# Expert stage of a token tower: the next group's rows turned, rounded and split in the middle of the gate products, and the scatters placed singly

## The reference

```python
logits = x @ router_w.T
routing_weights, selected = sparsemixer_eval(logits, JITTER_EPS)      # two experts a token
...
dense_w = dense_w.at[tok, selected[:, 0]].add(routing_weights[:, 0])
dense_w = dense_w.at[tok, selected[:, 1]].add(routing_weights[:, 1])
out = jnp.zeros_like(x)
for e in range(E):
    h = jax.nn.silu(x @ w_gate[e].T) * (x @ w_up[e].T)
    out = out + dense_w[:, e:e + 1] * (h @ w_down[e].T)
```

## Time and profile before

| | us |
|---|---|
| median of 3 runs | 2599.9 (2595.83 to 2601.3) |
| the profiled execution | 2601.53 |
| its span, first to last instruction | 2599.8 |
| PE busy in the span | 2218.6 |
| DVE / ACT / POOL busy | 1842.9 / 1715.3 / 1743.4 |
| mean granted clock of TensorE | 0.93 of full speed |

### The profile page before, as it was taken

One profiled execution on the slowest core, in us unless ns is written; L12 is line 12 of the kernel. 1 busy time (PEld: TensorE's weight loads), 2 busy tenths in 40 slices (PEclk: granted clock), 3 DMA queues, 4 the chain that ended last, 5 costly groups with the idle time before them and its releaser, 6 DMA issues. The chain is left out here.

```text
span 2599.8 us, 37397 instructions
## 1 busy us (share of the span) xinstructions
PE 2218.6 (85%) x11394; PEld 1850.5 (71%) x11394; DVE 1842.9 (71%) x3736; ACT 1715.3 (66%) x3574; POOL 1743.4 (67%) x1528
## 2 busy tenths in 40 slices
PE   0177578999999999999999999999999993838885
PEld 0064436887878788787888878788888882728885
DVE  2656457788878778887878878778787773465553
ACT  3433306787777878787787777878878783216663
POOL 4145507878787777878778787877777774017884
PEclk9975568999999999999999999999999997759998
DMA  9856717244343334524234442313312203426776
GB/s 380 336 200 221 243 38 201 70 98 123 86 121 81 94 93 95 136 73 124 75 94 107 96 133 54 80 40 63 68 30 56 47 14 92 139 85 191 197 197 174
DMA packets 199860, 314.81 MB, mean 121 GB/s; under 512 B 95915, under 2 KB 130219, under 8 KB 186731
## 3 DMA queue, kind: packets, MB, share of 16 engines
q1 hardware_dynamic: 189947, 298.23, 40.5%
q0 software_dynamic: 9712, 14.18, 2.9%
HBM read 210.20 MB, written 101.75 MB: 120 GB/s over the span
## 5 line engine op out<-in xcount | busy, mean ns | idle before, releaser
L1419 POOL TENSOR_TENSOR p_lo<-prob,p_hi 128x512 fp32r<-128x512 f32 (+3 forms) x1056 | 1211.4, 1166 | 376.7 <-ACT p_hi L1503 352.5
L1501 ACT ACTIVATE prob<-ps_s 128x512 f32<-128x512 f32 (+4 forms) x1344 | 726.9, 541 | 347.2 <-DVE ps_s L1741 169.3
L1503 ACT ACTIVATE p_hi<-ps_s 128x512 fp32r<-128x512 f32 (+3 forms) x1344 | 727.1, 541 | 1.6
L1638 DVE TENSOR_REDUCE max_part<-ps_x 128x1 f32<-128x512 f32 x744 | 506.4, 686 | 55.7 <-PE ps_x L1550 46.2
L1636 DVE CUSTOM_DVE_ANT_0 ps_x<-ps_x,before 128x128 f32<-128x128 f32 x496 | 244.3, 493 | 33.9 <-PE ps_x L1550 25.6
L1603 PE MATMUL ps_o<-p_hi,v_lat 128*128 128x512 f32 (+3 forms) x640 | 244.2, 382 | 17.5 <-POOL p_lo L1419 17.2
L1603 PE MATMUL ps_o<-p_hi,v_win 128*128 128x512 f32 (+3 forms) x640 | 237.1, 371 | 3.4 <-POOL p_lo L1419 3.4
L1605 PE MATMUL ps_o<-p_lo,v_win 128*128 128x512 f32 (+3 forms) x640 | 235.2, 368 | 0.0
L1605 PE MATMUL ps_o<-p_lo,v_lat 128*128 128x512 f32 (+3 forms) x640 | 234.4, 366 | 0.0
L1741 DVE TENSOR_TENSOR ps_s<-ps_s,mask_kq 128x128 f32<-128x128 f32 x512 | 153.6, 300 | 110.9 <-PE ps_s L1522 104.2
L1419 DVE TENSOR_TENSOR p_lo<-prob,p_hi 128x512 fp32r<-128x512 f32 (+1 forms) x224 | 191.3, 854 | 46.0 <-ACT p_hi L1503 40.2
(11 more groups left out here) (433 smaller groups left out, 5796.4 us busy)
## 6 DMA issues: line engine op xcount, KB each, us to landing
raw<-in_experts_w_dram SPq DMA_DIRECT2D x23, 1536.0 KB, 7.4
wbuf<-in_tok_weight_dram SPq DMA_DIRECT2D x16, 2000.0 KB, 16.9
head_first<-kw_scratch SPq DMA_DIRECT2D x72, 256.0 KB, 5.0
kw_scratch<-st_hi SPq DMA_DIRECT2D x48, 256.0 KB, 2.3
kw_scratch<-st_lo SPq DMA_DIRECT2D x48, 256.0 KB, 3.0
q_scratch<-st_hi SPq DMA_DIRECT2D x48, 256.0 KB, 3.2
q_scratch<-st_lo SPq DMA_DIRECT2D x48, 256.0 KB, 3.8
head_first<-q_scratch SPq DMA_DIRECT2D x48, 256.0 KB, 5.8
```

Of the source, the lines that this page charges most:

```text
L1419: ns.tensor_tensor(upper if low else p_lo[:, i % LSLOTS, c:CH], prob[low:P, i % NPROB, c:CH], upper.bitcast(F32), ALU.subtract).then_inc(s ...
L1501: nc.scalar.activation(prob[low:P, i % NPROB, c:CH], ps_s[i % 3][low:P, c:CH], ACT.Exp, scale=SCALE).then_inc(s["p_full"], 1)
L1503: nc.scalar.activation(p_hi[:, i % SLOTS, c:CH], ps_s[i % 3][:, c:CH], ACT.Exp, scale=SCALE).then_inc(s["p_up"], 1)
L1638: ins = nc.vector.tensor_reduce(mpart[:, q, c:c + 1], bank[:, 0:w], axis=AX.X, op=ALU.max)
```

## The change

Three things are moved; nothing is added to or taken from what is computed.

- The transposes for group i + 1, and with them `upper_x` and `lower_x`, move from the end of group i to before its third block (f = 2), on PE, ACT and DVE.
- `upper_gate` and `lower_gate` for group i + 1 move one block later: f = 1, 2 and 3 do blocks 0, 1 and 2, and block 3 follows behind the last `hm` (DVE) or before the last `h_hi` (ACT).
- `scatter` handles one half (q), and waits for that half's `yw` alone. The two scatters of group i - 2 are issued in group i behind the second and the third `h_lo`; before, those of group i - 1 stood together at the end of group i. The last two groups' scatters come together at the end, as before.

```diff
--- before.py
+++ after.py
@@ -2170,14 +2170,13 @@
                                                  in_offset=bass.IndirectOffsetOnAxis(ap=g.slot_tok[:, n:n + 1], axis=0)
                                                  ).then_inc(s[f"xg{i % 2}"], 16)
 
-            def scatter(i):
-                pool.wait_ge(s["yw"], HT * (i + 1))
-                for q in range(HT):
-                    n = HT * i + q
-                    if i:
-                        pool.wait_ge(s[f"add{q}"], 16 * i)
-                    nc.gpsimd.indirect_dma_start(out=g.acc_dram[q], out_offset=bass.IndirectOffsetOnAxis(ap=g.slot_tok[:, n:n + 1], axis=0),
-                                                 in_=yw[:, i % 2, q, :], in_offset=None, compute_op=ALU.add).then_inc(s[f"add{q}"], 16)
+            def scatter(i, q):
+                pool.wait_ge(s["yw"], HT * i + q + 1)
+                n = HT * i + q
+                if i:
+                    pool.wait_ge(s[f"add{q}"], 16 * i)
+                nc.gpsimd.indirect_dma_start(out=g.acc_dram[q], out_offset=bass.IndirectOffsetOnAxis(ap=g.slot_tok[:, n:n + 1], axis=0),
+                                             in_=yw[:, i % 2, q, :], in_offset=None, compute_op=ALU.add).then_inc(s[f"add{q}"], 16)
             gather(0)
             gather(1)
             for i in range(NTL):
@@ -2187,9 +2186,11 @@
                     nc.gpsimd.tensor_tensor(h_lo[:, i % 2, f, :], hm[:, n % 2, :], h_hi[:, i % 2, f, :].bitcast(F32), ALU.subtract).then_inc(s["lo"], 1)
                     if f == 0 and i + 2 < NTL:
                         gather(i + 2)
-                if i:
-                    scatter(i - 1)
-            scatter(NTL - 1)
+                    if f in (1, 2) and i >= 2:
+                        scatter(i - 2, f - 1)
+            for i in (NTL - 2, NTL - 1):
+                for q in range(HT):
+                    scatter(i, q)
 
         @block.tensor
         def _(pe):
@@ -2208,6 +2209,8 @@
                 pe.wait_ge(s["xlo"], i + 1)
                 pe.wait_ge(s["wlo"], gate_split(i, 3))
                 for f in range(FB):
+                    if f == 2 and i + 1 < NTL:
+                        x_transposes(i + 1)
                     n = FB * i + f
                     cols = slice(f * P, (f + 1) * P)
                     for ps, m, sem, free in ((ps_g, 0, "g", "silu"), (ps_u, 2, "u", "hm")):
@@ -2236,8 +2239,6 @@
             x_transposes(0)
             for i in range(NTL):
                 gate_up(i)
-                if i + 1 < NTL:
-                    x_transposes(i + 1)
                 if i:
                     down(i - 1)
             down(NTL - 1)
@@ -2281,6 +2282,8 @@
                 upper_gate(0, f)
             for i in range(NTL):
                 for f in range(FB):
+                    if f == 2 and i + 1 < NTL:
+                        upper_x(i + 1)
                     n = FB * i + f
                     act.wait_ge(s["g"], n + 1)
                     if n >= 2:
@@ -2290,11 +2293,11 @@
                         upper_down(i)
                     if f:
                         upper_h(i, f - 1)
-                    if i + 1 < NTL:
-                        upper_gate(i + 1, f)
+                    if f and i + 1 < NTL:
+                        upper_gate(i + 1, f - 1)
+                if i + 1 < NTL:
+                    upper_gate(i + 1, FB - 1)
                 upper_h(i, FB - 1)
-                if i + 1 < NTL:
-                    upper_x(i + 1)
                 if i:
                     weigh(i - 1)
             weigh(NTL - 1)
@@ -2318,6 +2321,8 @@
                 lower_gate(0, f)
             for i in range(NTL):
                 for f in range(FB):
+                    if f == 2 and i + 1 < NTL:
+                        lower_x(i + 1)
                     n = FB * i + f
                     dve.wait_ge(s["silu"], n + 1)
                     dve.wait_ge(s["u"], n + 1)
@@ -2326,10 +2331,10 @@
                     nc.vector.tensor_tensor(hm[:, n % 2, :], sg[:, n % 2, :], ps_u[n % 2][:, 0:TOK], ALU.mult).then_inc(s["hm"], 1)
                     if f == 0:
                         lower_down(i)
-                    if i + 1 < NTL:
-                        lower_gate(i + 1, f)
+                    if f and i + 1 < NTL:
+                        lower_gate(i + 1, f - 1)
                 if i + 1 < NTL:
-                    lower_x(i + 1)
+                    lower_gate(i + 1, FB - 1)
             for j in range(NJ):
                 c = slice(4 * j, 4 * j + 4)
                 dve.wait_ge(s[f"fin{j}"], 16 * HT)
```

## The result

| | before | after |
|---|---|---|
| median, us | 2602.06 (9 runs, 2595.83 to 2603.23) | 2609.24 (9 runs, 2606.55 to 2612.15) |
| ratio to before | 1 | 1.0031, 95% interval 1.002 to 1.0041 |
| profiled execution's span, us | 2599.8 | 2607.1 |

The changed kernel is slower by 0.31%: 8 us by the ratio, 7.2 between the medians. That is more than the 0.2% that a measurement tells from nothing, and small.

A forecast was written before the change was run, and what follows sets the result against it. POOL's round with DVE/POOL port exclusion was taken as the bound: 8.88 + 1.14 + 0.38 + 0.26 = 10.66, taken as 10.6 against 10.54 us a group. With the ends, +2.2 us on the median 2599.9: 2602, range 2581 to 2616.

The forecast's parts named there:

- What bounds the group: Expert stage: PE waits through a loop that closes over POOL, which is idle only 1.04 of 10.54 us a group.
- POOL's own work, 8.88: POOL's h_lo's, gathers and scatters with gaps, without exclusion, after the change: 8.88 us a group.
- The three collisions of the main case: POOL waits for DVE's two-operand splits: 1.14 us at a group's first h_lo, 0.38 and 0.26 at the gathers.
- main case: Steady group as summed: 10.6 us against 10.54, gate products at 2.57 after the second h_lo's start; chance 0.52.
- The collision at the last split: DVE's split for f = 3 against the h_lo behind the first scatter: split goes first, 0.10 us ahead, costing nothing.
- A: Zero of the group's clock in the forecast: the start of a group's second h_lo on POOL, in us.
- second rival: The h_lo behind the first scatter takes the port ahead of the last weight split: +15 us, 2615; chance 0.22.
- The Trainium skill's rule: A two-SBUF-input DVE instruction and a GpSimd one reading SBUF contend for ports: group stays at 10.6, without it 9.3.
- First rival, exclusion no dearer than before: Large split meets POOL inside a scatter, so POOL loses about 0.68: 9.56 us a group, 2582; chance 0.26.
- Costed at nothing: Moved transposes (0.35 us on PE either way), weight loads, scatter and yw waits add no time.
- The ends of the stage: Intervals outside the steady pace: first with scatters -0.7, last whole +0.7, last group +0.9, first two +0.1 each.
- the case without any exclusion: Within the faster rival: PE's 9.32 us a group is the bound, 19 x -1.22 + 1, giving 2579.

The follow-up runs named there:

- e3: Changed kernel with DVE's weight splits reading a zero tile in PSUM in place of the rounded weights; 0.9892 of before, 9.16 us a group.
- e10: Changed kernel with the PSUM zero tile as second operand in the last weight split (f = 3) alone; 0.9999 of before, 10.47 us a group.
- e7: Changed kernel with the two single scatters behind the third and fourth h_lo instead of the second and third; 0.9955 of before, 9.82 us a group.
- e11: Changed kernel with the PSUM zero tile as second operand in the large split (down block) alone; 1.0006 of before, 10.45 us a group.
- e9: Changed kernel with both scatters of group i-2 together behind the second h_lo; 1.0 of before, 10.52 us a group.
- e1: Kernel before with only the change's single scatters, rows and gate blocks as before; 0.9979 of before, 10.24 us a group.
- e2: Changed kernel without its single scatters, the pair at the group's end as before; 0.9996 of before, 10.35 us a group.
- e6: Changed kernel with h_lo computed by DVE instead of POOL; 0.9891 of before, 9.07 us a group.

## Why the prediction was right, and where its size was off

Forecast: 2602, +2.2 us, range 2581 to 2616, with 0.47 for no change that can be told and 0.27 for slower. Measured: 2609.2, +7.2 (by the interval of the ratio, 5 to 11). The median is in the range and the sign is that of the forecast, but the outcome is "slower", which I held for less likely than no change. The range was wide enough for both rivals, so that the time fell into it says little by itself; what speaks for the prediction is that the bound, the exclusion and the three collisions of its sum are found in the trace. A fourth collision was missing from the sum.

- **What bounds the group** (right). POOL's round with its collisions sets it before and after; e3 removes them and arrives at 9.16 where the sum without them said 9.3 at most for PE.
- **POOL's own work, 8.88** (right, and not what decides). The gap ahead of a scatter that stands singly is 0.17; I took 0.16.
- **The three collisions of the main case** (right in place, a little large): about 1.0, 0.29 and 0.20 against 1.14, 0.38 and 0.26. Of the 1.0, 0.17 is the wait for h_hi and only some 0.8 the exclusion.
- **The collision at the last split** (the term that was mis-sized, at nothing). I had the last split free at A+1.82 because it asks 0.10 ahead of the h_lo behind the scatter, and put the other outcome into the second rival, at 11.27 a group and 0.22. The split did ask first (A+1.83; the h_lo is shown from A+2.01) and was held off all the same, but only until about the scatter's end: it is through at A+3.28, and not at A+3.88, behind the whole h_lo, as the rival had it. Then the h_lo waited for the split. Gate products came at A+3.38: main case 2.57, rival 3.94. POOL's last h_lo of the group was through at A+6.39, and not at A+5.68: the 0.57 of this collision and the slightly longer scatters. The large split, ready at A+5.72, had to wait for it, so the 0.8 by which the gate products came late cost nothing more; POOL's 0.57 is what the group pays. The group is 11.00, between 10.6 and 11.27, by an outcome that I had not thought of, and it was luck that it lay between two that the range covered. e10 shows the price, 0.53 us a group, and its 10.47 is what the main case (10.6) stands for.
- **The Trainium skill's rule** ("SBUF — State Buffer", section "SBUF: two separate sides"), on which the main case and this rival lean by way of the rows: the trace agrees. In e3, with DVE's second operand in PSUM, the first h_lo takes 0.74 and not 1.52. The Trainium skill's section "Who interferes with whom" takes descriptor writing out of it for a tensor_tensor, as something inferred. Here the gathers take 1.01 and 0.98 in e3 against 1.28 and 1.19, so a gather is held up by a two-operand split; whether it is held for writing descriptors or for reading its index list, which lies in SBUF too, no run here shows.
- **First rival, exclusion no dearer than before** (wrong for this order, right as a mechanism): e7 is it, one place later, with the large split begun inside a scatter and 9.82 a group, where the rival had 9.56.
- **Costed at nothing** (right): the transposes stand 2.94 after the products' start without a wait, and no wait for raw or xg shows in the list.
- **The ends of the stage** (right as a sum). From the third group's start to the last group's, 18 intervals are at the steady pace (11.00 against 10.53), and they make 8.4 us where the forecast had 1.1. The last whole interval went from 9.16 to 9.59 (+0.4; I had +0.7; the 9.32 of the earlier trace rows is 9.16 when it is cut at the start of the last group's products, 0.16 earlier), the first one by -0.1 (I had -0.7), what lies ahead of it by -0.4 (I had +0.2) and what follows the last group's start by +1.3 (I had +0.9). These add up to +1.2 against my +1.1, so the whole error is in the steady group. In the two traces the stage is 9.6 us longer; the medians say 7.2.
- **Slips in the working.** PE's wait is 1.2 us a group and not "some 1.3" (21.9 us in 18 groups), and the case without any exclusion is 2578 from the median of 2599.9, not 2579. Neither enters the sum.

## What to carry to other kernels

Where DVE and POOL both read two operands from SBUF, write down for each instruction when it asks and who holds, also for instructions that wait behind a DMA issue on POOL; a move that shortens a dependency chain can lengthen the group by putting two such instructions side by side. Two halves of a change that each lose nothing can lose together, so a half that looks harmless is not proof. And a wait that is taken away can come back as another: price it by a run, not by its length (e11: 0.55 for a wait of 0.78). Before tuning the order around such an exclusion, ask whether the work can leave one of the engines: here, with DVE at 77% of the time afterwards, moving four small instructions of each group was worth two and a half times the best reordering tried (1.14% against 0.45%).

## What was not expected of the hardware

- An instruction with two SBUF operands that is queued on POOL behind a scatter holds DVE off from before it is shown as started (DVE's split from 0.90 after the scatter's start, h_lo shown from 1.08), and while the scatter still runs. With another scatter queued instead (e9), DVE is not held; nor is the split of e1, which begins 0.31 after the scatter's start and is through before the h_lo is shown. Then, at the scatter's end, DVE went first and the h_lo second, so the hold did not last through both. In the earlier trace rows, where the split began 0.06 after the h_lo was shown, it was the h_lo that went first. How it is handed over stays open; only its two prices were measured, 0.76 for DVE and 0.57 for POOL.
- In the timelines read here a gather or scatter is delayed only if it starts inside such a DVE instruction (1.28 for a gather started inside a split, 0.97 for the second gather of e1, inside which a split starts). The large split of e7 begins inside a scatter, and both take their bare time (1.57 and 1.23).
- The same code ahead of the expert stage reached it at 2319.7 us in one profiled execution and at 2338.1 in another (first transposes of after and of e10). Spans of single profiled executions cannot tell 0.3%. The steady group can: in the traces of before and after, the 18 steady intervals between group starts stay within 0.05 us of 10.53 and of 11.00. Not every kernel is so even (e2 has two intervals of 11.5, e6 one of 10.2), so the ratio of the medians is needed beside it.
